# Moving the mean and the epsilon of an RMS norm from the ScalarE square root to an instruction of its own on VectorE

## The reference, cut to what matters

```python
def _rmsnorm(t, w):
    var = jnp.mean(t * t, axis=-1, keepdims=True)
    return t * jax.lax.rsqrt(var + EPS) * w          # EPS = 1e-06

q = jnp.einsum('bsd,ed->bse', x, Wq).reshape(bsz, seqlen, HQ, D)
k = jnp.einsum('bsd,ed->bse', x, Wk).reshape(bsz, seqlen, HK, D)
v = jnp.einsum('bsd,ed->bse', x, Wv).reshape(bsz, seqlen, HK, D)
q = _rmsnorm(q, q_norm_w)
k = _rmsnorm(k, k_norm_w)
q = _rope(q, pos)
k = _rope(k, pos)
```

## Time and profile before

| | |
|---|---|
| median of three runs | 2418.71 us |
| the profiled execution: its own time | 2418.48 us |
| its span, first to last instruction | 2416.6 us |
| busy in the span: PE / DVE / ACT / POOL | 2372.4 / 1814.1 / 1315.5 / 721.5 us |
| the stretch 170 to 694 us (projection of queries and keys), busy: PE / DVE / ACT / POOL | 524.00 / 473.30 / 311.53 / 327.58 us |

### The profile page before, as it was taken

How to read it: one execution, slowest core, us unless ns; L and a number is a source line. 1 busy time by engine, 2 the same in 40 slices (tenths; PEclk the granted TensorE clock), 3 DMA queues, 4 the chain that set the end, 5 groups by cost and what they waited for, 6 DMA issues and landing times. The chain is left out here.

```text
span 2416.6 us, 53476 instructions
## 1 busy us (share of the span) xinstructions
PE 2372.4 (98%) x16044; PEld 2155.6 (89%) x16044; DVE 1814.1 (75%) x3145; ACT 1315.5 (54%) x3697; POOL 721.5 (30%) x713
## 2 busy tenths in 40 slices
PE   5999999999999999999999999999999999999999
PEld 4888888888888999999999999999999998888877
DVE  6659999999942788877888777887778876666653
ACT  3335665666533676766676766767667761111120
POOL 2006666666621222222222222222222214131100
PEclk8999999999999999999999999999999999999999
DMA  9633333333347788878888788887888888666622
GB/s 346 232 122 97 96 99 101 114 98 100 99 154 240 245 297 295 291 276 291 297 298 292 279 286 298 294 300 279 284 293 301 295 273 290 213 221 201 216 70 105
DMA packets 433668, 542.35 MB, mean 224 GB/s; under 512 B 36532, under 2 KB 349652, under 8 KB 429012
## 3 DMA queue, kind: packets, MB, share of 16 engines
q1 hardware_dynamic: 390852, 398.43, 48.0%
q0 software_dynamic: 36864, 134.23, 15.9%
q10 hardware_dynamic: 5904, 9.06, 1.1%
HBM read 440.59 MB, written 101.01 MB: 224 GB/s over the span
## 5 line engine op out<-in xcount | busy, mean ns | idle before, releaser
L1344 DVE CUSTOM_DVE_ANT_0 at_sm<-ps,at_mask 128x544 f32<-128x544 f32 x512 | 369.2, 721 | 253.6 <-PE ps L1241 245.1
L1275 PE MATMUL ps<-at_pt,at_v_raw 128*128 128x128 f32 x4096 | 540.8, 275 | 0.0
L1275 PEld LDWEIGHTS ps<-at_pt,at_v_raw 128*128 128x128 f32 x4096 | 497.6, 192 | 0.0
L1404 ACT ACTIVATE at_pt<-ps 128x512 f32<-128x512 f32 x512 | 304.2, 594 | 294.9 <-PE ps L1250 192.6
L1417 ACT ACTIVATE at_pr<-at_sm,at_nm 128x544 f32<-128x544 f32 x512 | 384.3, 751 | 66.2 <-DVE at_nm L1344 65.7
L952 POOL TENSOR_TENSOR pr_m<-pr_qn,tb 128x256 f32<-128x256 f32 x320 | 327.6, 1043 | 298.2 <-DVE pr_qn L921 294.8
L1331 DVE TENSOR_TENSOR at_k_lo<-shared,at_k_hi 128x1088 fp32r<-128x1088 f32 x256 | 325.8, 1273 | 0.0
L774 PE MATMUL ps<-pr_hi,xh 128*128 (+1 forms) x768 | 316.0, 411 | 0.5 <-ACT pr_stage L907 0.5
L1196 POOL DMA_INDIRECT at_v_raw<-v_cache,at_idx x256 | 277.9, 1086 | 113.4 <-issue 61.9
L1250 PE MATMUL ps<-constants,at_pr 128*128 128x128 f32 x2048 | 306.5, 272 | 0.1
L776 PE MATMUL ps<-pr_hi,xl 128*128 (+1 forms) x768 | 303.4, 395 | 0.0
(11 more groups left out here) (236 smaller groups left out, 4184.5 us busy)
## 6 DMA issues: line engine op xcount, KB each, us to landing
shared<-k_t SPq DMA_DIRECT2D x1024, 128.0 KB, 4.2
qk_t<-pr_stage SPq DMA_DIRECT2D x160, 256.0 KB, 2.2
shared<-qk_t SPq DMA_DIRECT2D x64, 512.0 KB, 7.5
o_t<-at_ot SPq DMA_DIRECT2D x64, 512.0 KB, 6.8
o_raw<-o_t SPq DMA_DIRECT2D x32, 1024.0 KB, 5.8
shared<-ri_d SPq DMA_DIRECT2D x32, 1024.0 KB, 8.0
f_w<-wqkv SPq DMA_DIRECT2D x12, 1024.0 KB, 5.6
s_k_in<-k_cache SPq DMA_DIRECT2D x16, 512.0 KB, 7.7
```

The source lines that it names most:

```text
L1275: e.matmul(sums(w, k), v_raw[:, q, c, g * D:(g + 1) * D], pt[:, jj % 4, c * P:(c + 1) * P], start=(k == 0 and c == 0), stop=False, skip_gr ...
L1344: e.tensor_tensor_reduce(out=sm[:, r, :], in0=scores(r), in1=mask[:, q, :], scale=-SC, scalar=3e38, op0=ALU.add, op1=ALU.min, accum_out=nm ...
L1404: e.activation(pt[:, jj % 4, :], ps_w(jj % 2), ACT.Copy).then_inc(s_pt, 1)
```

## The change

The scale and the bias leave the square root. VectorE gets a new instruction in front of its step: for unit u-2 it computes `ss = ss * (1/128) + 1e-6` in place, on 128x4 numbers, and raises a new semaphore `s_ms`. The square root then has neither scale nor bias and waits for `s_ms`. The squares of unit u-1 wait for `s_ms` of unit u-2 in place of ACT's own `s_red`. The column of constants that held the epsilon goes.

```diff
-C_EPS = C_MOD + 1
 ALIGN = 32
-C_ALL = C_EPS + 1
+C_ALL = C_MOD + 1
...
-    c[:, C_EPS] = EPS
...
-        s_proj, s_red, s_rt, s_rs, s_qn, s_m1, s_m2, s_qr, s_t, s_stage = (
-            sem(n) for n in ("proj", "red", "rt", "rs", "qn", "m1", "m2", "qr", "t", "stage"))
+        s_proj, s_red, s_ms, s_rt, s_rs, s_qn, s_m1, s_m2, s_qr, s_t, s_stage = (
+            sem(n) for n in ("proj", "red", "ms", "rt", "rs", "qn", "m1", "m2", "qr", "t", "stage"))
...
 # @block.scalar
                 if live(1):
                     m, r = u - 1, (j - 1) % 4
-                    wait(e, s_red, m)
+                    wait(e, s_ms, m)
                     e.wait_ge(s_proj, m + 1)
...
                 if live(2):
                     m, r = u - 2, (j - 2) % 4
-                    e.wait_ge(s_red, m + 1)
-                    e.activation(rt[:, r, :], ss[:, r, :], ACT.Sqrt, bias=cst[:, C_EPS:C_EPS + 1], scale=1.0 / D).then_inc(s_rt, 1)
+                    e.wait_ge(s_ms, m + 1)
+                    e.activation(rt[:, r, :], ss[:, r, :], ACT.Sqrt).then_inc(s_rt, 1)
...
 # @block.vector
             def step(i, j, u, live):
+                if live(2):
+                    m, r = u - 2, (j - 2) % 4
+                    e.wait_ge(s_red, m + 1)
+                    e.tensor_scalar(ss[:, r, :], ss[:, r, :], 1.0 / D, EPS, ALU.mult, ALU.add).then_inc(s_ms, 1)
                 if live(3):
```

## The result

The changed kernel takes 2434.78 us (median of 4 runs, 2432.28 to 2435.87) where the kernel before, in the same comparison, takes 2419.24. The ratio is 1.006, with a 95% interval of 1.0049 to 1.0073: slower by 15.5 us. All 27 runs of the changed kernel on record lie between 2431.71 and 2437.12, with a median of 2434.46. The forecast was 2433.5 in a range of 2417 to 2446.

A forecast was written before the change was run, and what follows sets the result against it. TensorE set the projection's pace; VectorE would become the bound, 53.5 us against 51.7 in 16 steps, making unit 163 14.7 us late: 2418.5 + 14.7 = 2433.2, 2433.4 against the median, forecast 2433.5, range 2417 to 2446.

The forecast's parts named there:

- The room of VectorE: Projection: VectorE needs 45.7 us in 16 steps against TensorE's 51.7, leaving 6.0 us, 0.38 a step.
- The one price that the trace did not show: Head of VectorE's step: new instruction waits for GpSimd's second product, costing 0.62 us without a low half of weights, bounds 0.09 to 0.75.
- a low half in the same place: VectorE's instruction on a low half of the weights, just after `m1`: 1.23 us beside GpSimd, 0.68 in the median case.
- 198 ns row of the prologue: One-input TENSOR_SCALAR of 128x16 at 9.45: 198 ns beside a working GpSimd, 174 alone; taken as a sign of being held up.
- The size: VectorE's projection step becomes 3.19 us, or 3.81 with a low half; 528.2 us over 158 steps, unit 163 14.7 late.
- a step of the sum: Last `qn` ends at 705.3; the first matmul of unit 163 needs its bank, so it comes 14.7 us late.
- ScalarE's waits at no cost: Squares waiting for VectorE's step cost 0: ScalarE needs 1.82 to 2.48 us, under 3.19, with 0.7 in hand.
- The cheaper root: ScalarE's root without scale and bias gains 0, since ScalarE waits for TensorE in nearly every unit.
- Nothing won back later: Values, attention and output hang on TensorE and move as a whole, so the projection's 14.7 us delay stays.
- The small instruction that isn't held up: Rival at the head of VectorE's step: 0.09 us a step, TensorE stays the bound, 2418.7 us; chance 0.25.
- The dearer one: Rival: reciprocal starts only after the new instruction's end and a semaphore's way, 0.11 a step, 17 us more, 2451; chance 0.07.
- The ring: Rival: VectorE and ScalarE wait for each other in turn; 40 steps at 0.3 us, 12 us more, 2446; chance 0.03.

The follow-up runs named there:

- e4_alone: Kernel before plus a TENSOR_SCALAR of 128x4 on a spare SBUF slice at the head of VectorE's step, waits unchanged: 2428.88 us, ratio 1.0055.
- e7_six: Kernel before plus six RECIPROCALs of 128x4 on spare SBUF slices at the head of VectorE's step, waits unchanged: 2404.26 us, ratio 1.0003.

## Why the prediction was right, point by point

- **The room of VectorE.** 0.38 us a step, from the back-to-back steps. Shown: six reciprocals just fill it and cost nothing; 0.62 in three steps of four overfills it.
- **The one price that the trace did not show.** The argument went from a low half in the same place (1.23 against 0.68) and from a single 198 ns row of the prologue. Shown by the result (700 against 155 ns), and by three edits that each take away one condition: the SBUF result, GpSimd at work, GpSimd's long instruction. Each brings the time back to the kernel before. So the engines of this kernel do not meet only at semaphores, as the description at the start has it: VectorE and GpSimd also meet at SBUF. The Trainium skill (SBUF — State Buffer, section "SBUF: two separate sides") gives as the reason a lock on a pair of ports, which VectorE takes in a two-port mode. That fits the 700 against 155 ns and all three edits; that the instruction reads in such a mode is not shown directly. The PSUM experiment changes the manner of the write as well, so reading and writing are not told apart.
- **The size.** Forecast: 3.19 us in steps without a low half and 3.81 with one. Measured from `qn` to `qn`: 3.18 in the one and 3.77 in the other (401.61 to 404.79 to 408.56 in the rows after; over the loop 3.17 to 3.18 and 3.78, but 3.86 in 9 of the 39 steps with a low half). The second and the last `qn`:

```profile
178.19 0.69 DVE L923 TENSOR_TENSOR pr_qn<-ps,f_a 128x512 f32<-128x512 f32 x1
...
703.61 0.69 DVE L923 TENSOR_TENSOR pr_qn<-ps,f_a 128x512 f32<-128x512 f32 x1
```

  They are 525.4 us apart instead of 528.2, 2.8 less. The second `qn` comes 0.4 later than forecast after taking off the prologue's 1.4; why is not shown. And a step of the sum was wrong: it let unit 163 start at the end of the last `qn`, but that ends at 704.30 and unit 163 starts at 705.30, 1.0 later. Behind the last low half VectorE, at 3.17 us a step, is faster than TensorE, at 3.233: the last unit held up starts at 685.91, and the six up to unit 163 follow at TensorE's own pace. So 13.3 us of the projection stand against the 14.7 forecast (14.7 - 2.8 + 0.4 + 1.0). That unit 163 starts at the very 705.3 of the forecast is luck, by the prologue's 1.4. So is the closeness of the whole time, 1.3 above the forecast: the prologue and the spread between sessions (12.8 us slower in one, 15.5 in the other) are as large as that.
- **ScalarE's waits at no cost.** Shown by the waits alone. In the trace of the changed kernel the squares wait 225 us for VectorE instead of 201 for TensorE; it is the same idle time under another name, and e4_alone, as slow, shows 213 for TensorE.
- **The cheaper root.** It lasts 230 ns instead of 318 (medians of 160). ScalarE's busy time fell and nothing came of it, as forecast.
- **Nothing won back later.** The projection's delay is still there at the start of the values and of the attention (788.1 against 773.5). The attention's own length differs between executions by more than the whole effect (1188 to 1205 us), which the prediction did not reckon with; it would have misled whoever compared the spans of two single profiles.
- **The rivals.** The small instruction that isn't held up: false in SBUF, true to PSUM. (The reciprocal spoke for it less than the prediction has it: of the 160 before, 79 started beside a working GpSimd, not most of them; the 714 of e7_six do not depend on that.) The dearer one: false, the reciprocal starts 0.61 after the start of the held-up instruction, 0.09 before its end, as behind an unhindered one (408.30 + 0.16 to 408.37). The ring: it shows only with the instruction in the other place, as 0.2 us a step that nobody waits for.

## What to carry to other kernels

Before putting a small SBUF instruction such as this TENSOR_SCALAR on VectorE, look at what GpSimd does at that moment of the step, not at the number of elements: four numbers can wait 0.55 us. The kind of instruction matters too, since the reciprocal of the same size is never held up. Here the same instruction costs no time a few lines later in the step, or with its result in PSUM, or beside a GpSimd that works in short pieces. Count room in back-to-back steps, not in busy share: a held-up instruction counts as busy, so 97% can be harmless and 98% the bound.

## What the runs showed of the hardware that was not expected

- Small independent VectorE instructions follow each other by 0.07 us, though each lasts 0.14 to 0.16; one that waits for the semaphore of the one ahead follows by 0.20 (404.59 to 404.79).
- The kernel before took 2419, 2416 and 2404 us in three sessions. Where traces of a session exist, the attention carries the difference: from first to last score 1205.3 us in the first (kernel before), 1199.8 to 1201.3 in the four traces of the second, and 1188.5 to 1189.4 in the four of the third, one of them:

```profile
L1248 PE MATMUL ps<-at_k_hi,at_q_hi x1024: 285/299/384, 774.1 to 1962.8; 128*128 128x256 f32 x171
```

The projection, from unit 0 to unit 163, is 538.00 and 537.95 us in the two traces of the changed kernel. What sets the attention's length is open. The record names one chip (0) for the second session and another (14) for the third, so the chip may be what differs; no run tells it from the hour of the session.
